# A routed feed-forward kernel: routed rows turned on VectorE, biases moved, batch slots rearranged

## The chip, the cores and the metric

The kernel runs on one core of a Trainium2 chip. The metric is the device time of one launch in microseconds (us), the median of several launches. Five engines run side by side, each with a program of its own, and wait for one another by semaphores: TensorE (PE, with its weight loads as PEld), VectorE (DVE), ScalarE (ACT), GpSimd (POOL) and SyncE (SP, which only issues DMAs here).

## The reference

16 batches of 256 tokens with 256 features pass one block:

```python
x = x + tanh(g_xattn) * xattn(layernorm(x), ctx, ctx)   # 16 heads of 16, full softmax, biases
x = x + tanh(g_ffn) * ffn(layernorm(x))
# ffn
scores = softmax(xf @ w_router)                          # 8 experts, the best 2 of each token
h = silu(xf @ w1[e]) * (xf @ w3[e]);  y = h @ w2[e]      # 256 -> 512 -> 256
out = shared / 3 + 2/3 * sum over the two experts of score * y   # shared: the same form, for all tokens
```

## The kernel before

Everything is fp32; each operand of a large matmul is split into a high part of type fp32r and the rest, and `three` (lines 550 to 552) multiplies high by high, high by rest and rest by high. The program has two stages.

**Attention.** An iteration `i` works on several batches at once: `Eb` = i+4 (layer norm), `A` = i+3 (the projections of q, k and v), `B` = i+1 (row maxima of the scores), `C` = i, `S` = i-1, `S2` = i-2 (output projection, second layer norm), `S3` and `S4` (router, list positions, scatter of the rows into lists of experts in the DRAM tensor `xs_d`). Each iteration has 8 **slots** p = 0..7, and in each of them PE computes scores of one pair of heads for the exponentials (`scores_to_exp`, bank `bank_ss`), scores of another pair for the maxima (`scores_to_max`, `bank_sm`), and then what the table in the section on the change lists. Both score banks are single: the next slot's scores wait for ACT's exponentials (`probs`) and for DVE's maxima (`row_max`) of this slot. `late_pair` says which pair of heads a slot's exponentials belong to: the first LATE slots still serve the batch before. `values` multiplies the probabilities of four heads by v, in four 32-column strips of the array; `turn_...`, `transposes` and `attention_rows` are transposes by matmul with the identity. On each engine `before(p)` and `behind(p)` list what it does ahead of and behind its score work of slot p. The order is written by hand, and each engine keeps it strictly.

**Feed-forward.** 16 tiles of 256 tokens pass the shared expert, and tiles of 256 rows pass the eight routed ones: tiles 0 to 5 are shared, then 34 are routed, then 10 shared. In a tile PE runs `up1` (24 matmuls), for a routed tile `transpose_x(g + 1)` (4 transposes of the next tile's rows `xg` into the bank `psX`; with the one ahead of the loop 35 times), `up3` (24) and `down(g - 1)` (24). The other engines prepare: ACT copies the turned rows to `xg_h` (`x_high_routed`, when up3 has released it), DVE subtracts to get `xg_l` (`x_low_routed`), multiplies the gate (`gated`, into `gg`) and splits again (`g_low`). SP loads the rows of tile u+3 when `xt_ps` says that the rows before are turned; POOL scatters results to `y_d` and converts the next expert's weights (`cut`: lines 1590 and 1594). The last three batches' attention overlaps the first shared tiles.

Of the kernel before, what the change touches and what calls it, by code (L numbers as in the profile page):

```python
# [31 lines left out]
P = 128  # L32
# [7 lines left out]
R = 3  # L40
# [6 lines left out]
LATE = 2  # L47
# [15 lines left out]
SPLIT_AT = NB - 3  # L63
WSZ = 2 * EC * HID + FC * E
# [3 lines left out]
XW = E + 1  # L68

# [59 lines left out]
def build(nc, x, ctxT, gates, wT, bqk, bv, bo, wr, wall, cst, out):  # L129
    with ExitStack() as keep:  # L130
# [84 lines left out]
        with ExitStack() as m:  # L215
# [21 lines left out]
            xg = sb(m, "xg", [P, TS, XW])  # L237
# [54 lines left out]
        xg_in = sem("xg_in"); xs_in = [sem(f"xs_in{i}") for i in range(2)]; xt_ps = sem("xt_ps"); xh_ok = sem("xh_ok"); xl_ok = sem("xl_ok")  # L292
# [60 lines left out]
        def _(sp):  # L353
# [10 lines left out]
            sp.sem_inc(xg_in, EARLY * 16)  # L364
            sp.sem_inc(xt_ps, EARLY)
# [66 lines left out]

            def load_shared(j, done=None):
# [54 lines left out]
            sp.dma_start(xg[:, :, :], parts(xs_d, 0, TR)).then_inc(xg_in, 16)  # L488
            clear_behind(sp, (2, 4, 6), z_done)
            sp.wait_ge(xt_ps, EARLY + 1)  # L490
            sp.dma_start(xg[:, :, :], parts(xs_d, TR, TR)).then_inc(xg_in, 16)
# [52 lines left out]
        def _(pe):  # L544
# [14 lines left out]

            def transpose_x(g):  # L560
                pe.wait_ge(xg_in, g * 16 + 16)
                pe.wait_ge(xl_ok, g)
                for t in range(TS):
                    for k in range(EC):
                        r = pe.transpose(psX[:, k * TR + t * P:k * TR + (t + 1) * P], xg[:, t, k * P:(k + 1) * P], ident)
                r.then_inc(xt_ps, 1)
# [143 lines left out]
            def one(i):  # L710
                A, B, C, S, S2, S3 = (stage(i, k) for k in (3, 1, 0, -1, -2, -3))

                for p in range(PAIRS):
# [5 lines left out]
                    if p == 0 and C and not among_first(C, 1):  # L719
                        turn_max(C, S2)  # L720
                    if p == 0 and S:
                        values(S, 2)
# [11 lines left out]
                    if p == 2 and S:  # L734
                        values(S, 3)
                    if p == 2 and A:
# [27 lines left out]
                    if p == 4 and C:  # L764
                        values(C, 0)
                    if p == 5 and S:
                        if A:
                            pe.wait_ge(xnTl_ok, A.n(1, 1))
                        elif S2:
                            pe.wait_ge(oTl_ok, S2.n(1, 1))  # L770
                        if S2:
                            pe.wait_ge(x2_ok, S2.n(1, 1))
# [1014 lines left out]
```

## Time and profile before

| | us |
|---|---|
| median of 3 runs (lowest to highest) | 838.9 (836.05 to 838.96) |
| the profiled execution's own time | 837.43 |
| its span, first to last instruction | 835.7 |
| PE busy in the span | 787.9 (94%) |
| DVE, POOL, ACT busy | 518.1 (62%), 422.7 (51%), 414.9 (50%) |

The span is 1.7 us shorter than the execution. In rows of the profile, a time is in us from the span's start, `x4` merges four like instructions that follow each other, and a bracket says how long the engine was idle before and what released it. Lines (L550) are those of the kernel before.

### The profile page before, as it was taken

The page shows a single profiled execution, that of the slowest core. Times are in us where ns is not written, and L with a number is a line of the kernel's source. Part 1 is how long each engine was busy: PE and PEld are TensorE (multiplying, and loading weights), DVE is VectorE, ACT ScalarE, POOL GpSimd, SP SyncE.
Part 4 walks back from the last instruction along what each step waited for, and adds up shares of the span by engine and source line. Part 5 has one row for each costly group of instructions (what it writes and reads, how often), then busy time and mean ns, then how long its engine had stood idle before and what let it go on. Part 6 is the DMA issues. An engine that isn't in the chain of part 4 may idle for free.

```text
span 835.7 us, 19335 instructions
## 1 busy us (share of the span) xinstructions
PE 787.9 (94%) x7073; PEld 703.0 (84%) x7074; DVE 518.1 (62%) x1084; ACT 414.9 (50%) x690; POOL 422.7 (51%) x486
## 2 busy tenths in 40 slices
PE   4689999999999998789999999999999999999997
PEld 4556777777777775568999999999999999999996
DVE  6567889998888888847653334333433332346787
ACT  5657777777777776453334433333333333333331
POOL 5533446666666653466672567465836482236000
PEclk9889999999999999689999999999999999999999
DMA  6844556766666652244487233223323312118522
GB/s 219 275 142 164 172 191 212 237 229 216 207 217 215 206 186 84 69 164 153 138 248 270 77 113 115 76 79 122 101 82 96 99 57 69 51 51 325 215 75 76
DMA packets 100542, 127.37 MB, mean 152 GB/s; under 512 B 17664, under 2 KB 82432, under 8 KB 100480
## 3 DMA queue, kind: packets, MB, share of 16 engines
q1 hardware_dynamic: 86336, 80.37, 30.2%
q0 software_dynamic: 14144, 46.19, 16.2%
q8 instruction: 37, 0.61, 0.3%
q14 instruction: 25, 0.20, 0.1%
HBM read 75.36 MB, written 50.91 MB: 151 GB/s over the span
## 4 chain that ended last, share of the span: by engine, by line
PE 80%; DVE 6%; issue 4%; DMA 4%; ACT 3%; POOL 2%; SPq 1%; POOLq 0%; DVEq 0%; ACTq 0%
PE bank L550 9%; PE bank L551 8%; PE bank L552 8%; PE bank L634 6%; PE bank_ss L605 6%; PE bank_sm L550 5%; PE bank_sm L552 5%; PE bank_sm L551 5%; PE bank_ss L550 5%; PE bank_ss L552 5%; PE bank_ss L551 5%; PE bank_sm L618 4%; PE bank L641 3%; DMA y_rows<-xs_d 2%; DVE row_max L1238 2%
## 5 line engine op out<-in xcount | busy, mean ns | idle before, releaser
L1238 DVE TENSOR_REDUCE row_max<-bank_sm 128x4 f32<-128x1024 f32 x124 | 151.6, 1222 | 43.2 <-PE bank_sm L618 42.0
L943 ACT ACTIVATE probs_T<-bank_ss 128x1024 f32<-128x1024 f32 x123 | 126.6, 1029 | 21.3 <-PE bank_ss L605 20.2
L1217 DVE TENSOR_TENSOR gT_l<-gg,gT_h 128x1024 fp32r<-128x1024 f32 x49 | 66.0, 1348 | 89.0 <-ACT gT_h L1074 87.7
L550 PE MATMUL bank_ss<-xg_h,w_h 128*128 128x256 f32 x400 | 115.9, 290 | 0.0
L550 PE MATMUL bank_sm<-xg_h,w_h 128*128 128x256 f32 x400 | 113.5, 284 | 1.0 <-DVE xg_l L1217 1.0
L552 PE MATMUL bank_sm<-xg_l,w_h 128*128 128x256 f32 x400 | 112.9, 282 | 0.0
L551 PE MATMUL bank_sm<-xg_h,w_l 128*128 128x256 f32 x400 | 112.9, 282 | 0.0
L552 PE MATMUL bank_ss<-xg_l,w_h 128*128 128x256 f32 x400 | 112.8, 282 | 0.0
L551 PE MATMUL bank_ss<-xg_h,w_l 128*128 128x256 f32 x400 | 112.7, 282 | 0.0
L550 PE MATMUL bank<-w_h,gT_h 128*128 128x256 f32 x392 | 111.0, 283 | 0.4 <-DVE gT_l L1217 0.4
L551 PE MATMUL bank<-w_h,gT_l 128*128 128x256 f32 x392 | 110.9, 283 | 0.0
L552 PE MATMUL bank<-w_l,gT_h 128*128 128x256 f32 x392 | 110.7, 282 | 0.0
L1644 POOL TENSOR_TENSOR qk_s<-qk_s 128x512 fp32r<-128x512 f32 x32 | 41.8, 1307 | 113.4 <-ACT qk_s L984 113.4
L1217 DVE TENSOR_TENSOR xg_l<-bank,xg_h 128x512 fp32r<-128x512 f32 x34 | 23.5, 693 | 120.9 <-ACT xg_h L1062 120.9
L1068 ACT ACTIVATE sg<-bank_sm 128x512 f32<-128x512 f32 x98 | 53.3, 596 | 67.7 <-PE bank_sm L552 67.7
L1723 POOL DMA_INDIRECT y_d<-y_s,y_rows x68 | 73.0, 1074 | 19.0 <-issue 17.4
L550 PEld LDWEIGHTS bank_sm<-xg_h,w_h 128*128 128x128 f32 x400 | 76.3, 191 | 1.9 <-DVE xg_l L1217 1.4
L984 ACT ACTIVATE qk_s<-bank,bqk_s 128x256 f32<-128x256 f32 (+1 forms) x128 | 53.5, 481 | 47.9 <-PE bank L552 47.9
L551 PEld LDWEIGHTS bank_sm<-xg_h,w_l 128*128 128x128 f32 x400 | 76.4, 191 | 0.0
L552 PEld LDWEIGHTS bank_sm<-xg_l,w_h 128*128 128x128 f32 x400 | 76.3, 191 | 0.0
L551 PEld LDWEIGHTS bank_ss<-xg_h,w_l 128*128 128x128 f32 x400 | 76.2, 191 | 0.0
L1721 POOL TENSOR_TENSOR go<-go 128x1 f32<-128x1 f32 x34 | 11.7, 345 | 127.3 <-ACT y_s L1084 100.7
(200 smaller groups left out, 2079.2 us busy)
## 6 DMA issues: line engine op xcount, KB each, us to landing
qk_d<-qk_s SPq DMA_DIRECT2D x64, 256.0 KB, 2.2
w_raw<-wall POOLq DMA_DIRECT2D x27, 512.0 KB
k<-qk_d SPq DMA_DIRECT2D x48, 256.0 KB
q<-qk_d SPq DMA_DIRECT2D x48, 256.0 KB
xg<-xs_d SPq DMA_DIRECT2D x35, 257.0 KB
y_pairs<-y_d POOLq DMA_DIRECT2D x16, 512.0 KB, 8.8
x<-x SPq DMA_DIRECT2D x16, 256.0 KB, 4.9
c_s<-ctxT SPq DMA_DIRECT2D x16, 256.0 KB, 2.9
```

The lines of the kernel that those rows point to most:

```text
L550: pe.matmul(out, ah, bh, start=first and k == 0, stop=False)
L551: pe.matmul(out, al, bh, start=False, stop=False)
L552: r = pe.matmul(out, ah, bl, start=False, stop=last and k == n - 1)
L605: r = pe.matmul(exp_bank(V.b, pv)[:, par * 512 + half * L:par * 512 + (half + 1) * L], k4[V.slot][own, pv, half * P:(half + 1) * P], q4[V. ...
L634: r = pe.matmul(OT[g % 2][PVW * i:PVW * (i + 1), :], v_s[V.v_slot][:, kc, h, :], pT[:, h % 8, kc * L:(kc + 1) * L], start=kc == 0, stop=kc ...
L943: act.activation(pT[:, 2 * (pv % 4):2 * (pv % 4) + 2, :].rearrange("p h t -> p (h t)"), exp_bank(V.b, pv)[:, :], ACT.Exp, scale=D ** -0.5) ...
L984: r = act.activation(dst.bitcast(F32) if half else dst, bnk[:, oc * L:(oc + 1) * L], ACT.Identity, bias=bqk_s[:, 2 * side + oc:2 * side + ...
L1068: r = act.activation(sg[:, 2 * n:2 * n + 2, :].rearrange("p f t -> p (f t)"), psH1[n][:, :], ACT.Silu)
L1217: return v.tensor_tensor(dst, ps, high.bitcast(F32), ALU.subtract)
L1238: v.tensor_reduce(mx[B.slot][:, :, :].rearrange("p t (r q) -> p r t q", r=2)[:, :, :, p], max_bank(B.b, p)[:, :].rearrange("p (r t k) -> p ...
L1644: po.tensor_tensor(rest, rest.bitcast(F32), high.bitcast(F32), ALU.subtract).then_inc(done, 1)
L1723: po.indirect_dma_start(out=yd, out_offset=bass.IndirectOffsetOnAxis(ap=to[:, t:t + 1].bitcast(U32), axis=0), in_=y_s[:, t, :], in_offset= ...
```

## The change

Four things change.

1. **Routed rows are turned on DVE.** `transpose_x` goes. SP loads a tile by four DMAs of 64 columns each, to 32 partitions each, in pieces of 256 bytes (before: one DMA in pieces of 1028 bytes). DVE turns the tile by one transpose in blocks of 32 by 32 (`turn_rows`) from `xq` to `xrT`, both in SBUF. The rows of w1 and w3 are put in the order that this gives. `x_high_routed` and `x_low_routed` read `xrT` in place of the PSUM bank.
2. **Biases move.** POOL's `add_bias` of batches 11 to 15 stood at the start of iterations 13, 14 and 15; 11 and 12 now stand behind the first scatter of iteration 12, and 13 to 15 behind that of iteration 13.
3. **The slots of a batch are rearranged**, with LATE 3 in place of 2:

| slot | PE behind the scores, before | after |
|---|---|---|
| 0 | turn_max(C), values(S,2) | values(S,1) |
| 1 | logits, project k | turn_max(C), logits, project k |
| 2 | values(S,3), transposes of xn | values(S,2) |
| 3 | project_out, rank | transposes of xn, project_out, rank |
| 4 | values(C,0) | values(S,3) |
| 5 | attention_rows(S), project q | project q, attention_rows(S) |
| 6 | values(C,1), turn_out(S) | values(C,0) |
| 7 | project v, turn_norm(S2) | project v, turn_out(S), turn_norm(S2) |

4. **ACT and DVE follow.** ACT: the copy of the maxima goes from ahead of slot 0's exponential to ahead of slot 1's, the copy of v from ahead of slot 0's to behind it, the two halves of q from around slot 6's to behind slot 5's, the high part of the output from ahead of slot 7's to behind it. DVE: `residual_variance` and `divide` go from ahead of the maxima of slots 5 and 6 to behind them, `residual` and `score_sum`/`score_weights` to behind those of slots 4 and 3. The last batch has one exponential and one `values` more behind the loop.

```diff
-LATE = 2
+LATE = 3
+LAST_X = NB - AHEAD
+BIAS_AT = {LAST_X: (LAST_X - 1, LAST_X), LAST_X + 1: (NB - 3, NB - 2, NB - 1)}
+QD = 32
+FQ = E // (P // QD)
...
+            def load_tile(r):
+                for fg in range(P // QD):
+                    sp.dma_start(xq[QD * fg:QD * (fg + 1), :, :],
+                                 xs_d[bass.ds(r, TR), FQ * fg:FQ * (fg + 1)].rearrange("(t p) d -> p t d", p=QD)).then_inc(xg_in, 16)
...
             def load_routed(u):
                 r = tile_row(u)
-                sp.wait_ge(xt_ps, u + EARLY)
-                sp.dma_start(xg[:, :, :], parts(xs_d, r, TR)).then_inc(xg_in, 16)
+                sp.wait_ge(xt_ok, u + EARLY)
+                load_tile(r)
...
                 up1(g, p)
-                if routed:
-                    transpose_x(g + 1)
                 up3(g, p)
...
+            def turn_rows(g):
+                v.wait_ge(xg_in, g * 64 + 64)
+                v.wait_ge(xl_ok, g)
+                v.transpose(xrT[:, :, :].rearrange("p c (t q) -> p c t q", q=QD),
+                            xq[:, :, :].rearrange("p t (c j) -> p c t j", c=EC)).then_inc(xt_ok, 1)
             def x_low_routed(g):
+                turn_rows(g)
                 v.wait_ge(xh_ok, g + 1)
-                low(xg_l[:, :, :], psX[:, :].rearrange("p (c t) -> p c t", c=EC), xg_h[:, :, :]).then_inc(xl_ok, 1)
+                low(xg_l[:, :, :], xrT[:, :, :], xg_h[:, :, :]).then_inc(xl_ok, 1)
...
-                if S2:
+                if S2 and S2.b <= LAST_X - 2:
                     add_bias(S2)
-                if i == NB - 1:
-                    add_bias(Batch(NB - 2))
-                    add_bias(Batch(NB - 1))
...
                 if S4:
                     scatter(S4, 0)
+                if i in BIAS_AT:
+                    for b in BIAS_AT[i]:
+                        add_bias(Batch(b))
```

PE, the first two slots of an iteration of the attention stage, before (`bank_ss` and `bank_sm` are the scores, `row_max` is turn_max, `probs_T` is values, `wr_s` the router's logits):

```order
L605 MATMUL bank_ss<-q_2,k_2 128x256 x4
L618 MATMUL bank_sm<-k_1,q_1 128x256 x4
L672 MATMUL bank<-consts,row_max 16x128 x2
L634 MATMUL bank<-probs_T,v 32x256 x8
L605 MATMUL bank_ss<-q_2,k_2 128x256 x4
L618 MATMUL bank_sm<-k_1,q_1 128x256 x4
L696 MATMUL bank<-wr_s,xn2T 128x8 x4
```

and the same two slots after, on the same engine:

```order
L608 MATMUL bank_ss<-q_2,k_2 128x256 x4
L621 MATMUL bank_sm<-k_1,q_1 128x256 x4
L637 MATMUL bank<-probs_T,v 32x256 x8
L608 MATMUL bank_ss<-q_2,k_2 128x256 x4
L621 MATMUL bank_sm<-k_1,q_1 128x256 x4
L675 MATMUL bank<-consts,row_max 16x128 x2
L699 MATMUL bank<-wr_s,xn2T 128x8 x4
```

The turning of the maxima has moved past the values and the next slot's scores.

POOL, before, from iteration 14's last scatter to iteration 15's first (`x<-x,gated_bo` is the bias):

```order
L1629 CAST xn_1<-consts 128x2
L1603 TENSOR_TENSOR spare_p<-spare_p 128x1
L1633 DMA xs_d<-xn_1,slot_i 36864x257 x2
L1618 TENSOR_TENSOR x<-x,gated_bo 128x512 x3
L1629 CAST xn_2<-consts 128x2
L1603 TENSOR_TENSOR spare_p<-spare_p 128x1
L1633 DMA xs_d<-xn_2,slot_i 36864x257 x2
```

and after, where the three biases stand in iteration 13:

```order
L1620 TENSOR_TENSOR spare_p<-spare_p 128x1
L1650 DMA xs_d<-xn_0,slot_i 36864x257 x2
L1635 TENSOR_TENSOR x<-x,gated_bo 128x512 x3
L1629 TENSOR_TENSOR rstd<-bn_mv,power 128x2
L1646 CAST xn_0<-consts 128x2
L1620 TENSOR_TENSOR spare_p<-spare_p 128x1
```

The three biases now stand between a first scatter and the root of the second norm, two iterations earlier.

DVE, the loop over routed tiles, before:

```order
L1217 TENSOR_TENSOR xg_l<-bank,xg_h 128x512
L1405 REGISTER_ALU
L1409 TENSOR_TENSOR gg<-sg,bank_ss 128x512 x2
L1217 TENSOR_TENSOR gT_l<-gg,gT_h 128x1024
L1504 REGISTER_ALU
```

and after:

```order
L1413 STREAM_TRANSPOSE xrT<-xq 128x512
L1418 REGISTER_ALU
L1225 TENSOR_TENSOR xg_l<-xrT,xg_h 128x512
L1426 TENSOR_TENSOR gg<-sg,bank_ss 128x512 x2
L1225 TENSOR_TENSOR gT_l<-gg,gT_h 128x1024
```

The transpose heads the loop, right behind the last `gT_l` of the tile before, and the subtraction reads SBUF in place of a bank.

## Rows read from the trace of the kernel before

**Rows 1.** Windows: length, busy PE, PEld, DVE, ACT, POOL, granted clock, DMA, GB/s.
```profile
183.35:304.33 120.98, 118.77 (x1248) 91.28 (x1249) 106.93 (x276) 88.27 (x161) 75.54 (x92) 1.00 0.61 204
...
322.40:325.60 3.20, 3.20 (x26) 1.41 (x24) 2.43 (x6) 1.55 (x3) 0.00 (x0) 0.53 0.02 5
342.50:356.10 13.60, 12.70 (x74) 8.52 (x75) 8.72 (x25) 6.12 (x9) 3.65 (x5) 0.50 0.11 40
...
424.00:734.00 310.00, 308.58 (x2584) 308.18 (x2584) 114.29 (x152) 112.83 (x175) 168.85 (x178) 1.00 0.35 106
```
**Rows 2.** Timeline of PE around the transposes of routed rows: start, us, instruction.
```profile
507.58 0.60 PE L565 MATMUL bank<-consts,xg 128*128 128x128 f32 x4
508.14 0.28 PE L551 MATMUL bank_ss<-xg_h,w_l 128*128 128x256 f32 x1
...
516.64 0.60 PE L565 MATMUL bank<-consts,xg 128*128 128x128 f32 x4
```
**Rows 3.** Timeline of PE, first matmul of two shared tiles in a row.
```profile
766.10 0.28 PE L550 MATMUL bank_sm<-xg_h,w_h 128*128 128x256 f32 x1
...
774.68 0.28 PE L550 MATMUL bank_sm<-xg_h,w_h 128*128 128x256 f32 x1
```
**Rows 4.** Timelines of DVE and ACT in the same routed tile.
```profile
506.56 1.23 DVE L1217 TENSOR_TENSOR gT_l<-gg,gT_h 128x1024 fp32r<-128x1024 f32 x1 [1.96 <-ACT gT_h L1074]
...
511.14 0.60 ACT L1062 ACTIVATE xg_h<-bank 128x512 fp32r<-128x512 f32 x1 [2.20 <-PE bank_ss L552]
511.77 0.69 DVE L1217 TENSOR_TENSOR xg_l<-bank,xg_h 128x512 fp32r<-128x512 f32 x1 [3.99 <-ACT xg_h L1062]
```
**Rows 5.** Timelines at the first routed tiles, and the DMA of 4 MB.
```profile
427.62 1.29 DVE L1409 TENSOR_TENSOR gg<-sg,bank_ss 128x512 f32<-128x512 f32 x2 [1.98 <-PE bank_ss L552]
430.25 0.28 PE L550 MATMUL bank_sm<-xg_h,w_h 128*128 128x256 f32 x1
431.60 1.95 DVE L1217 TENSOR_TENSOR gT_l<-gg,gT_h 128x1024 fp32r<-128x1024 f32 x1 [2.09 <-ACT gT_h L1074]
440.12 1.19 POOL L1713 DMA_DIRECT2D x_all<-x_d  x1
442.96 0.39 SPq L503 DMA_DIRECT2D xg<-xs_d  x1
452.48 0.66 PE L565 MATMUL bank<-consts,xg 128*128 128x128 f32 x4 [1.06 <-DMA xg<-xs_d]
...
x_all<-x_d POOLq DMA_DIRECT2D x1, 4096.0 KB, 16.9
```
**Rows 6.** Timeline of PE in one iteration: starts of slot 1, values in slot 4, slot 5.
```profile
205.26 0.51 PE L605 MATMUL bank_ss<-q,k 64*128 64x256 f32 x4 [0.37 <-issue]
205.60 0.40 PE L618 MATMUL bank_sm<-k,q 63*128 63x256 f32 x4
...
213.72 1.07 PE L634 MATMUL bank<-probs_T,v 128*32 128x256 f32 x16
214.72 0.51 PE L605 MATMUL bank_ss<-q,k 64*128 64x256 f32 x4
215.13 0.50 PE L618 MATMUL bank_sm<-k,q 63*128 63x256 f32 x4
```
**Rows 7.** Timelines of DVE, POOL and PE at the ends of iterations 13 and 14.
```profile
319.18 2.24 DVE L1304 TENSOR_SCALAR xn<-x_s,bn_mv,rstd 128x256 f32<-128x256 f32 x2
321.51 0.63 PE L641 MATMUL bank<-consts,xn 128*128 128x128 f32 x4 [1.63 <-issue]
...
338.63 4.67 DVE L1304 TENSOR_SCALAR xn<-x_s,bn_mv,rstd 128x256 f32<-128x256 f32 x2
339.10 3.71 POOL L1618 TENSOR_TENSOR x<-x,gated_bo 128x512 f32<-128x512 f32 x3
343.40 1.08 PE L641 MATMUL bank<-consts,xn 128*128 128x128 f32 x4 [4.06 <-issue]
```
**Rows 8.** Timeline of DVE at the end of an early iteration.
```profile
138.08 1.70 DVE L1304 TENSOR_SCALAR xn<-x_s,bn_mv,rstd 128x256 f32<-128x256 f32 x2 [0.46 <-POOL rstd L1612]
```

More of the change, by code:

```diff
@@ L718, in one @@
                         scores_to_max(B, p)
-                    if p == 0 and C and not among_first(C, 1):
+                    if p == 0 and S:
+                        values(S, 1)
+                    if p == 1 and C and not among_first(C, 1):
                         turn_max(C, S2)
-                    if p == 0 and S:
-                        values(S, 2)
                     if p == 1 and S3:
@@ L734, in one @@
                     if p == 2 and S:
-                        values(S, 3)
-                    if p == 2 and A:
+                        values(S, 2)
+                    if p == 3 and A:
                         pe.wait_ge(xn_ok, A.n(1, 1))
@@ L788, in one @@
                             project(q_bank(A), 0, oc, xnT_h, xnT_l, q_ps)
+                    if p == 5 and S:
+                        if A:
+                            pe.wait_ge(xnTl_ok, A.n(1, 1))
+                            if among_first(A, R):
+                                pe.wait_ge(qh_ok, A.n(1, 1))
+                        elif S2:
+                            pe.wait_ge(oTl_ok, S2.n(1, 1))
+                        if S2:
+                            pe.wait_ge(x2_ok, S2.n(1, 1))
+                        if among_first(S, 1):
+                            pe.wait_ge(gbo_ok, 1)
+                        if C:
+                            pe.wait_ge(mT_ok, C.n(1, 1))
+                        attention_rows(S)
                     if p == 6 and C:
-                        values(C, 1)
-                    if p == 6 and S:
-                        turn_out(S)
+                        values(C, 0)
                     if p == 7 and A and not among_first(A, R):
@@ L802, in one @@
                         r.then_inc(bo_ps, 1)
+                    if p == 7 and S:
+                        turn_out(S)
                     if p == 7 and S2:
@@ L812, in _ @@
             x13, x14, x15 = (Batch(NB - k) for k in (3, 2, 1))
+            scores_to_exp(x15, PAIRS - 3)
+            values(x15, 1)
             scores_to_exp(x15, PAIRS - 2)
+            logits(x13)
             scores_to_exp(x15, PAIRS - 1)
             values(x15, 2)
-            logits(x13)
             pe.wait_ge(lgc_ok, x13.n(1, 1))
@@ L849, in _, with tile @@
                 up1(g, SHARED)
-                if g == EARLY - 1:
-                    transpose_x(EARLY)
                 up3(g, SHARED)
                 down(g - 1, SHARED)
-            def tile(g, p, before, routed=True):
+            def tile(g, p, before):
                 up1(g, p)
-                if routed:
-                    transpose_x(g + 1)
                 up3(g, p)
@@ L884, in _ @@
             end, = expert(NX - 1, 1, 0, value(T_B, NX - 1, EARLY + 2, EARLY + NT - 2), 1)
-            tile(end, SHARED, 1, routed=False)
+            tile(end, SHARED, 1)
             with pe.Fori(end + 1, end + (NB - 1 - EARLY)) as g:
-                tile(g, SHARED, SHARED, routed=False)
+                tile(g, SHARED, SHARED)
             final = end + (NB - 1 - EARLY)
@@ L1329, in before @@
                         best_two(S3)
-                    if p == 4 and S2:
+                    if p == 4 and S3:
+                        positions(S3, rk_p)
+                    if p == 4 and S2 and not A:
                         residual(S2)
-                    if p == 5 and S2:
-                        residual_variance(S2)
-                    if p == 6 and S:
-                        divide(S)
                     if p == 7 and S2:
```

125 lines of the change are left out of this document (59 added, 66 removed).

## The prediction, made before the changed kernel was run

> **What bounds the kernel.** I read the page's busy times first (they are in the table above): PE works in 787.9 of 835.7 us, the others in 62% or less. Then the same by stretches [rows 1]: in the routed tiles (424 to 734) PE is busy for 308.6 of 310.0 us and DVE for 114.3, so that what PE issues is the time. In six steady attention iterations PE is busy for 118.8 of 121.0 us, but DVE for 106.9 and ACT for 88.3: PE's order sets the time, and DVE has 2.3 us an iteration to spare. In two short stretches the granted clock is half (342.5 to 356.1) or nearly so (322.4 to 325.6). Last come the timelines at these places. Each of them stands at a wait of PE, of 1.63 and of 4.06 us, which the part on the biases takes up.
>
> **Transposes off PE.** Four transposes begin at 507.58, and the second matmul behind them at 508.14. Routed matmuls follow each other at 0.12 us: a tile takes 516.64 - 507.58 = 9.06 us, and (9.06 - 0.44)/72 = 0.12. Without the four, that second matmul would stand at 507.70, so they cost 0.44 us [rows 2]. From the other side: a shared tile with the same 72 matmuls takes 774.68 - 766.10 = 8.58 us [rows 3], which makes it 0.48. I take 0.44; 35 times that is **-15.4** us (at 0.48, -16.8).
>
> **What hides the turning on DVE.** No row shows a DVE transpose. The nearest is DVE's subtraction on as many elements (128x512), 0.69 us [rows 4]; I take that for the transpose. Free, it would be 0; for the other end I take 2.5 us, about four such passes. It starts when `gT_l` ends, 506.56 + 1.23 = 507.79, and ACT wants its result at 511.14, where up3 lets `xg_h` go [rows 4]: 3.35 us of room, 2.9 with the tile 0.44 shorter. Then ACT takes 0.60 and DVE 0.69, up to 512.46, while the next up1 starts 24 matmuls of `down` after up3, at about 513.7. Both ends of the transpose's cost fit, so in the loop it costs 0.
>
> The subtraction itself now has both inputs in SBUF. Such an operation can wait for POOL: `gT_l` took 1.95 us at 431.60 and 1.23 at 506.56 [rows 4, 5], 0.7 more, where POOL was converting weights. The room ahead of up1 is 1.3 us, so this is 0 too, with up to 0.5 at some of the 21 conversions as its worst end. The Trainium skill ("SBUF — State Buffer", the part on the shared port pair) says that a DVE operation with two SBUF inputs, or one in a two-port mode, and a GpSimd operation lock each other out for the whole instruction. By that rule the wait could be a whole conversion instruction, and the transpose might meet it as well; the trace agrees as far as 0.7 us goes.
>
> **The way into the routed tiles.** Here the room is missing. Before, `xg_l` of tile 6 followed `gg`, which ends at 428.91, while its turning was long done; up1 starts at 430.25 [rows 5]. After, the transpose stands between: 0.69 on DVE, 0.60 on ACT, 0.69 on DVE, so `xg_l` ends at 428.91 + 1.98 = 430.9 at best, 431.7 if it waits 0.7 for POOL. Up1 would want it at 430.25 - 0.44 = 429.8. I take **+1.5** (1.1 to 1.9).
>
> Then the load of tile 9. Before, it was issued at 442.96 and let PE go at 452.48, 9.5 us later: POOL had put 4 MB on the same DMA engines at 440.1, which land 16.9 us after it, at 457 [rows 5]. After, the load is issued 2 to 3 us later (behind the transpose of tile 8, which stands behind `gT_l` and three small router steps) and in four times as many pieces. I let it land with the 4 MB, at 457. With 0.69 + 0.60 + 0.69 behind it, up1 of tile 9 can start at 459.0. Before, that up1 stood behind the transposes of 452.48 and 48 matmuls, at 452.48 + 0.44 + 5.76 = 458.7. Less four transposes (1.8) and the wait of 1.06 that go, plus the 1.5 of above, PE asks for it at 457.3 and waits 1.7 us; against the 1.06 removed that is **+0.6**. If the pieces take the load's turn one by one beside the large ones and it ends later, up to +5. The Trainium skill ("DMA: Bandwidth & Descriptors", its table of numbers) says that a transfer wants pieces of 512 bytes or more for the full rate. By it every routed load is slower; elsewhere a whole tile of 8.6 us lies between issue and use, so only the rival on the entry gets its chance from it.
>
> **The biases.** DVE's normalisation is two instructions of 0.37 to 0.41 us. At 338.63 the pair took 4.67 us: it ended when the three biases, 339.10 + 3.71 = 342.81, were done, and PE's transposes waited 4.06 us for it. At 319.18 it took 2.24 us beside one bias, and PE waited 1.63 [rows 7]. After, no bias stands there: **-5.7**. Both waits end in slow clock. In 342.5 to 356.1 PE is busy for 12.7 us at half clock, at full clock 6.4; but DVE has 8.7 us to do in the same stretch [rows 1], so at most 4.0 to 6.4 come back, and I take 4.0. In 322.4 to 325.6 it is 3.2 us of nearly half clock: 1.5. Together **-5.5** (0 if the clock falls all the same). The three biases, now in iteration 13 behind the first scatter, meet small DVE operations with two SBUF inputs (the router's weights, now in slot 3). One bias is 1.24 us (3.71/3): +0.5, from 0 to 3.7. Behind the last batch PE waits for short chains of DVE and ACT, which do not get shorter; of the sum of 10.7 I let **+1.0** be lost there.
>
> **The slots.** In a steady iteration (20.16 us: 120.98/6) the one gap of PE is ahead of slot 1: 0.37 us [rows 6], since ACT copies the maxima ahead of slot 0's exponential. After, that copy waits beside logits and a projection: about -0.4. Against it: the scores behind a `values` take longer. At 214.72 they start 1.00 us after `values`, and the maxima's scores follow 0.41 later, at 205.26 0.34 later [rows 6]; with the like loss at the next step, some 0.17 in all. Before, one slot of eight pays that (the slot behind the gap doesn't), after, slots 1, 3, 5 and 7 do: +0.5. ACT now does both halves of q, four activations, ahead of slot 6's exponential: +0.2. DVE in the short slots (two times scores and one `values`, 0.34 + 0.33 + 1.00 = 1.67 us) has 1.2 us of maxima and up to 0.7 of statistics; the queue catches up in the long ones. Sum +0.3, which I take as 0 (-0.5 to +0.5, times 9). In the three iterations near 138 to 183 the normalisation takes 1.70 us [rows 8], the maxima of slot 7 come late and slot 0 pays some 0.5 us; after, POOL's subtraction of q stands a slot earlier and turn_max has left slot 0: **-1.5**.
>
> **Sum.** -15.4 + 1.5 + 0.6 - 5.7 - 5.5 + 0.5 + 1.0 + 0 - 1.5 = -24.5. The profiled execution took 837.43: 812.9. It stands 1.5 below the median, so 814.4 on the median's scale; I say **814.5**.
>
> **Rivals.**
> - *The clock falls all the same at the end of attention* (a wait of 1 us somewhere else in the last three iterations, where PE has less work than DVE). For it: DVE is busy for 8.7 us there. The 5.5 stay: 820.
> - *The entry jams*: tile 9's load runs on behind the 4 MB, PE stands for 5 us and more, and the clock halves for a while (another 2 to 4). 814.5 + 4 + 3: 821.5. For it: 9.5 us for 257 KB already before; against it: the 4 MB end at 457 in any case.
> - *The slots gain*: the gap goes and nothing comes, and DVE no longer meets POOL: 0.6 an iteration in 12, 807.
> - *Slower*: DVE and ACT cannot hold the short slots. Four slots of 1.67 us stretch to the 2.4 us that maxima plus another DVE step of 0.7 need with their hand-overs, and nothing is given back: 4 x 0.7 = 2.8 us an iteration, in 13 iterations +36: 851. It turns the sign from 24/13 = 1.9 us an iteration. Against it: DVE's load of 17.8 us an iteration (106.93/6) is the same as before and under 20.16.
> - *It does not do what it says*: the transpose is late in every tile and PE waits 0.44 or more for it. That needs over 2.9 + 1.3 us for one transpose, more than my upper end: 830 and up.
>
> **Chances.** My forecast 0.45 (its own range 810 to 819), clock 0.18, entry 0.13, slots gain 0.14, transpose late 0.04, slower 0.06. Range **804 to 828**, which leaves out some 2 in 10. A run of this kernel can't tell less than about 0.5%, 4 us, from no change. Faster by more: 0.92; within: 0.03; slower: 0.05.
>
> **What would show it.** PE without the line of `xg`'s transposes and a period of 8.6 us in routed tiles. DVE's transpose near 0.7 us and ending before ACT's wait for up3. One wait of PE before tile 6 and one before tile 9. Normalisations near 0.8 us a pair in iterations 13 and 14, and full clock from 322 to 356. Steady iterations at 20.2 us, with no gap ahead of slot 1. The prediction is wrong if PE waits for `xg_l` in the loop, if iterations grow by over 1 us, or if the clock falls at other places.

## The result and the profile after

| | before | after |
|---|---|---|
| median, us | 838.2 (836.05 to 838.96) | 828.0 (824.41 to 829.56) |
| ratio, 95% interval | | 0.9876 (0.9838 to 0.9914) |
| span of the profiled execution | 835.7 | 825.8 |

The change is faster by 1.2%, 10.2 us. I had said 814.5, in a range of 804 to 828: the sign is right, the size is less than half of the predicted 24. On a later occasion (e9) the ratio was 0.9917 (0.9904 to 0.993), some 7 us; the two intervals still overlap. Medians in this document are of all executions, while the ratios leave out one execution each of e2 (1471.92 us), e7 (842.51) and e15 (833.82) that lay over 1.5% above the fastest of its kernel.

First come the busy times and stretches of the kernel after; they answer to [rows 1].

```profile
PE 771.2 (93%) x6933; PEld 691.5 (84%) x6934; DVE 546.3 (66%) x1118; ACT 419.2 (51%) x690; POOL 431.1 (52%) x486
...
core 0: us, PE busy (x) PEld busy (x) DVE busy (x) ACT busy (x) POOL busy (x), PEclk, DMA share, GB/s
188.60:308.50 119.90, 119.20 (x1251) 93.00 (x1250) 106.80 (x275) 90.53 (x161) 76.97 (x94) 1.00 0.62 206
322.40:325.60 3.20, 2.64 (x33) 1.55 (x33) 2.89 (x11) 2.35 (x3) 2.09 (x4) 1.00 0.00 0
342.50:356.10 13.60, 11.85 (x127) 8.09 (x128) 12.69 (x45) 9.92 (x16) 6.45 (x9) 1.00 0.24 82
424.00:734.00 310.00, 304.44 (x2501) 303.05 (x2501) 143.82 (x184) 115.48 (x179) 178.31 (x181) 0.99 0.39 106
```

Six steady iterations take 119.90 us, 19.98 each (before 20.16; in the traces of e5 to e16 many of the changed ones take 20.1). The granted clock is full in both stretches at the end of attention where it was 0.53 and 0.50, and the normalisations there take 0.73 us, where they had taken 2.24 and 4.67 [rows 7]. In the routed tiles, where PE was busy for all but 1.4 of 310 us, it now stands still for 5.6. So both large steps of the prediction did what they should, and something else takes the time. To find it, cut both spans at instructions that both kernels have: PE's first, fourth and fourteenth `turn_max`, and the first matmuls of `up1` in tiles 0, 6 and 40 (the first shared one behind the routed). All from timelines of PE, one profiled execution each, us:

| kernel | ahead of 1st turn_max | to 4th | to 14th | to tile 0 | to tile 6 | routed, to tile 40 | rest |
|---|---|---|---|---|---|---|---|
| before | 42.7 | 57.6 | 204.0 | 66.3 | 59.6 | 310.3 | 95.2 |
| after | 43.2 | 63.2 | 202.1 | 56.8 | 63.4 | 301.9 | 95.2 |
| e9, the changed kernel again | 42.5 | 63.3 | 202.7 | 59.2 | 62.2 | 305.0 | 95.2 |
| e1, part 1 alone | 42.2 | 57.6 | 204.1 | 65.7 | 61.9 | 304.6 | 95.2 |
| e2, part 2 alone | 43.0 | 58.3 | 204.8 | 54.5 | 62.3 | 310.2 | 95.1 |
| e3, parts 3 and 4 alone | 42.3 | 62.5 | 202.2 | 54.7 | 62.7 | 310.6 | 95.2 |
| e10, parts 2 to 4 | 42.7 | 63.3 | 202.8 | 59.8 | 59.9 | 310.6 | 95.9 |
| e12, all mended | 43.0 | 62.2 | 202.6 | 56.2 | 60.3 | 295.1 | 95.3 |

DVE's timeline has the normalisation of iteration 14:

```profile
343.04 0.73 DVE L1312 TENSOR_SCALAR xn<-x_s,bn_mv,rstd 128x256 f32<-128x256 f32 x2
```

I had predicted nothing for the first three iterations; they take 5.6 us more. The routed tiles should have given 14.4 and gave 8.4. From the fourteenth turn_max to tile 0 came 9.5 of 10.7 us.

First the start: windows of PE at the low clock (length, busy PE, granted clock, DMA share, GB/s), after and then before.

```profile
43.50:50.30 6.80, 5.47 (x29) 0.50 0.71 230
53.70:60.50 6.80, 5.76 (x30) 0.50 0.20 56
```

```profile
45.50:48.90 3.40, 3.40 (x20) 0.50 0.63 197
52.40:55.80 3.40, 3.40 (x30) 0.50 0.54 156
```

Twice the half clock holds for 6.8 us in place of 3.4. ACT's timeline of the kernel after, and PE's, tell what PE waits for there:

```profile
52.48 0.60 ACT L958 ACTIVATE xnT_h<-bank 128x512 fp32r<-128x512 f32 x1 [1.59 <-PE bank L644]
52.98 1.02 ACT L945 ACTIVATE probs_T<-bank_ss 128x1024 f32<-128x1024 f32 x1
```

```profile
54.05 0.80 PE L608 MATMUL bank_ss<-q,k 64*128 64x256 f32 x4 [1.60 <-ACT probs_T L945]
```

ACT copies `xnT_h` ahead of slot 3's exponential, and the copy waits for PE's transposes, which the change has put behind the scores of that same slot. In a steady iteration slot 3 has project_out and rank to cover this. The first two iterations have neither, and the slot is short.

How long the half clock holds differs between traces of the same start. e5, e6 and e7 do not touch it and ran on one chip; they have 20.5, 13.6 and 10.2 us of half clock there, and the stretch to the fourth turn_max takes 65.1, 63.3 and 62.5 us. At like half clock, 10.2 us, it takes 58.3 with the old slots (e2) and 62.5 with the new (e3, e7). So some 4.2 of the 5.6 us come with the slots at like clock, and the rest with the half clock, of which every trace with the unmended new slots has 10.2 us or more (before and e1 6.8).

Between tiles 1 and 2 PE waits for the normalisation of the last batch, 2.37 us for 0.21 before; e7 takes this up:

```profile
390.11 0.44 PE L644 MATMUL bank<-consts,xn 128*128 128x128 f32 x2 [2.37 <-DVE xn L1312]
```

In iteration 13 stand the three moved biases. POOL, DVE and PE after:

```profile
313.46 3.75 POOL L1635 TENSOR_TENSOR x<-x,gated_bo 128x512 f32<-128x512 f32 x3
```

```profile
312.84 4.40 DVE L1267 TENSOR_TENSOR mask_total<-mask_total,mask 128x8 fp32r<-128x8 f32 x1
```

```profile
317.34 0.25 PE L709 MATMUL bank<-mask_total,counters 128*128 128x16 f32 x1 [2.59 <-issue]
```

One DVE addition of 8 numbers a partition (0.17 us in e3) takes 4.40: it begins 0.62 us ahead of POOL's three operations, under the issue of a scatter on POOL (312.45 to 313.44), and ends 0.03 us behind them. What held it before the biases began is not shown. It does not get its turn between two of them either. PE's rank matmuls read its result. In the trace of after the clock stays full behind this wait. In seven of the nine traces that have both the new slots and the moved biases (e4, e6 to e11) it doesn't: within some 2 us PE is at half clock for 3.4 us (in e9 from 319.2 to 322.6), in five of them once more 14 us later.

Last the routed tiles, first DVE in an undisturbed one:

```profile
497.70 1.23 DVE L1225 TENSOR_TENSOR gT_l<-gg,gT_h 128x1024 fp32r<-128x1024 f32 x1 [3.70 <-ACT gT_h L1080]
498.84 0.71 DVE L1413 STREAM_TRANSPOSE xrT<-xq 128x512 f32<-128x512 f32 x1
```

The transpose takes 0.7 us, PE no longer has the line of `xg`'s transposes, and the period is 8.64 us, for 9.06 in [rows 2]: as predicted. But at 428 and 490 two tiles are slow (tile 6 takes 10.20 us, tile 12 12.55), and four later starts of an expert (tiles 16, 21, 25 and 30) cost 0.5 to 0.8 us each. PE's waits at these two, and the clock behind them:

```profile
428.68 0.36 PE L561 MATMUL bank_sm<-xg_h,w_h 128*128 128x256 f32 x1 [1.84 <-DVE xg_l L1225]
490.85 0.58 PE L561 MATMUL bank<-w_h,gT_h 128*128 128x256 f32 x1 [2.27 <-DVE gT_l L1225]
```

```profile
429.20:432.60 3.40, 3.40 (x18) 0.50 0.62 176
490.60:494.00 3.40, 3.15 (x14) 0.50 0.72 211
```

The wait at 490.85 is followed back through ACT, POOL and SP of the kernel after:

```profile
487.49 0.60 ACT L1090 ACTIVATE y_s<-bank 128x512 f32<-128x512 f32 x1 [6.82 <-DMA y_d<-y_s,y_rows]
487.99 1.05 ACT L1080 ACTIVATE gT_h<-gg 128x1024 fp32r<-128x1024 f32 x1
```

```profile
485.07 0.99 POOL L1740 DMA_INDIRECT y_d<-y_s,y_rows  x1 [0.30 <-issue]
486.06 1.05 POOL L1607 CAST w_h<-w_raw 128x1024 fp32r<-128x1024 f32 x1
487.19 2.52 POOL L1611 TENSOR_TENSOR w_l<-w_raw,w_h 128x512 fp32r<-128x512 f32 x2
...
491.04 1.02 POOL L1740 DMA_INDIRECT y_d<-y_s,y_rows  x1 [0.19 <-issue]
```

```profile
487.64 0.39 SPq L520 DMA_DIRECT2D y_rows<-xs_d  x1
491.59 1.83 SPq L441 DMA_DIRECT2D xq<-xs_d  x4
496.27 0.39 SPq L520 DMA_DIRECT2D y_rows<-xs_d  x1
...
503.59 0.39 SPq L520 DMA_DIRECT2D y_rows<-xs_d  x1
```

The scatter of a tile's results lands; only then may ACT fill `y_s` again (and `gT_h` stands behind it on ACT, `gT_l` and PE's `down` behind that), and only then does SP load the next row numbers, without which POOL can't scatter. It is a circle. At 487.49 ACT has waited 6.8 us for it, since conversions of weights stand ahead of the scatter at an expert's start. From one load of row numbers to the next it is 8.6 us with a conversion in between (487.64 to 496.27) and 7.3 without (to 503.59), while a tile takes 8.64: a delay shrinks by 1.3 us a tile and not at all beside a conversion, and the next expert adds to it. The same loads before:

```profile
489.45 0.38 SPq L509 DMA_DIRECT2D y_rows<-xs_d  x1
497.01 0.38 SPq L509 DMA_DIRECT2D y_rows<-xs_d  x1
503.76 0.38 SPq L509 DMA_DIRECT2D y_rows<-xs_d  x1
```

There it was 7.6 us with a conversion and 6.75 without, under a tile of 9.07: a delay shrank by 1.5 and 2.3 us, and two tiles made it up. So the change took the room from both sides: the tile is 0.43 us shorter and the round 0.6 to 1.0 longer. Summed over the routed tiles, waits after and then before:

```profile
POOL go L1738 <- DMA y_rows<-xs_d: 83.8, 17, 16.4
ACT y_s L1090 <- DMA y_d<-y_s,y_rows: 69.6, 18, 6.8
```

```profile
POOL go L1721 <- DMA y_rows<-xs_d: 26.2, 4, 14.0
ACT y_s L1084 <- DMA y_d<-y_s,y_rows: 12.4, 3, 5.4
```

### The profile page after: what moved, and what is told of

Its sections match the earlier page's. It is cut to its first block, busy times and chain, and to the rows that moved or that the text cites. A ratio compares the mean times of both kernels' runs of the same rounds, so it can differ in the third digit from the quotient of the medians.

```text
span 825.8 us, 19358 instructions
## 1 busy us (share of the span) xinstructions
PE 771.2 (93%) x6933; PEld 691.5 (84%) x6934; DVE 546.3 (66%) x1118; ACT 419.2 (51%) x690; POOL 431.1 (52%) x486
## 4 chain that ended last, share of the span: by engine, by line
PE 56%; POOL 13%; DMA 11%; issue 8%; DVE 6%; ACT 4%; SPq 1%; POOLq 1%; ACTq 0%; DVEq 0%
PE bank_ss L608 6%; PE bank L637 6%; PE bank L561 6%; POOL w_l L1611 6%; PE bank L563 5%; PE bank L562 5%; DMA y_d<-y_s,y_rows 5%; PE bank_sm L621 5%; DMA y_rows<-xs_d 3%; PE bank_sm L561 3%; PE bank L644 3%; PE bank_sm L562 3%; PE bank_sm L563 3%; PE bank_ss L561 3%; PE bank_ss L563 3%
## 5 line engine op out<-in xcount | busy, mean ns | idle before, releaser
L561 PE MATMUL bank_ss<-xg_h,w_h 128*128 128x256 f32 x400 | 113.2, 283 | 0.0
L561 PEld LDWEIGHTS bank<-w_h,gT_h 128*128 128x128 f32 x392 | 75.4, 192 | 4.4 <-DVE gT_l L1225 4.4
L608 PEld LDWEIGHTS bank_ss<-q,k 64*128 64x128 f32 x492 | 38.2, 188 | 45.7 <-ACT probs_T L945 29.5
L563 PEld LDWEIGHTS bank_ss<-xg_l,w_h 128*128 128x128 f32 x400 | 76.4, 191 | 0.0
```

Source lines behind the costliest of these rows:

```text
L561: pe.matmul(out, ah, bh, start=first and k == 0, stop=False)
L563: r = pe.matmul(out, ah, bl, start=False, stop=last and k == n - 1)
L608: r = pe.matmul(exp_bank(V.b, pv)[:, par * 512 + half * L:par * 512 + (half + 1) * L], k4[V.slot][own, pv, half * P:(half + 1) * P], q4[V. ...
```

## The experiments

Eighteen runs, on five chips: e1 to e4, e5 to e8, e9 to e12, e13 to e16, and e17 with e18. Ratios are to the kernel before on the same chip, with 95% intervals. A time in the table above is one trace's.

### Parts of the change

e1 is part 1 of the change alone, e2 part 2 alone, e3 parts 3 and 4 alone, e10 parts 2 to 4; their edits are those of the numbered list in the section on the change.

> The kernel before with part 1 alone: routed rows turned on VectorE; biases and slots as before. Theory A (the routed stage loses its gain at the starts of experts, whatever stands in attention): period of a routed tile 8.64 us, but a slow tile at the entry (+3.4) and 4 to 8 us at the starts of experts, so about -7 us against before (831). Theory B (what I had predicted for this stage): -15.4 + 2.1, about -13 us (825).

Measured: 832.8 us, 0.9936 (0.9919 to 0.9953), 4.8 us. The routed tiles gain 5.7 us, the entry loses 2.3: theory A, if with less than its 7 us.

> The kernel before with part 2 alone: the biases of batches 11 to 15 moved, slots and routed tiles as before. Theory A: the waits of 1.63 and 4.06 us and the half clock behind them go (-11.2), the three biases in iteration 13 cost +2.7 and a little is lost behind the last batch: -7 to -9 us (830). Rival B (the slot rearrangement is needed for the clock to stay full): the waits go, the clock still falls somewhere in the last three iterations: -3 to -5 us.

Measured: 830.45, 0.9905 (0.9883 to 0.9926), 7.1 us. To tile 0 it gains 11.8 us where the waits and the half clock stood, and loses 2.7 on the way to tile 6. The clock stays full there without the new slots: theory A.

> The kernel before with parts 3 and 4 alone (slots rearranged, exponentials a slot later). Theory A (it is this part that lengthens the first iterations): +3 to +4 us in the first three iterations, -0.18 us in each of 9 steady iterations, +1 to +2 behind the last batch: together +2 to +5 us (841 to 843), and one more step of half clock near 42 to 59 us than before. Rival B: the slots are neutral at the start and gain 0.2 us an iteration: -2 us (836).

Measured: 831.53, 0.9928 (0.9911 to 0.9944), a gain of 6.0 us: both theories were wrong. The start costs 4.9 us, as A said. But the stretch to tile 0 gains 11.6, as much as moving the biases does, with the biases where they were. Its DVE and POOL show why: the normalisation is through before the bias begins.

```profile
320.01 0.73 DVE L1318 TENSOR_SCALAR xn<-x_s,bn_mv,rstd 128x256 f32<-128x256 f32 x2
```

```profile
321.27 1.29 POOL L1634 TENSOR_TENSOR x<-x,gated_bo 128x512 f32<-128x512 f32 x1
```

> The kernel before with the slots and the biases changed (parts 2 to 4), routed tiles as before. Alone the biases gave -7.1 us and the slots -6.0. Theory A (both remove the same two waits of PE at 321 and 343 and the same half clock, so that the second adds nothing, and the three biases in iteration 13 now cost 3.5 us): less than either alone, -3 to -5 us (834). Rival B (the gains add up): -13 us (825).

Measured: 834.47, 0.9961 (0.9949 to 0.9973), 3.0 us: less than either alone, as A said. Parts 2 and 3 remove the same two waits; together they pay for it twice, at the start (5.7 us) and in iteration 13, so that the stretch to tile 0 gains 6.5 us and not 11.7. In that stretch stand the rank's wait (2.56 us) and, behind it, twice 3.4 us of half clock, which neither part has alone.

### Single mends of the changed kernel

e9 is the changed kernel itself. It shares its chip with e10 to e12 alone; the chips of e4 and of e5 to e8 have no run of the unedited changed kernel, so those runs can only be set beside e9's ratio and beside each other.

> The changed kernel itself, unchanged. The four runs before this one (ratios 0.991 to 0.992) all stand above the 0.9876 measured for the changed kernel on another occasion, and in their traces the middle iterations take 20.17 us where the first run of the changed kernel had 19.98. Theory A: the gain of the change itself varies by 0.3 to 0.4% between occasions (waits for DMAs in the routed tiles), so here it lies anywhere from 0.987 to 0.993, and only runs of one occasion may be compared. Rival B: it is 0.9876 again, and each of the three edits (turning earlier, rstd earlier, xnT_h later) cost 3 us.

Measured: 830.78, 0.9917 (0.9904 to 0.993). It fits theory A, 10 us on one occasion and 7 on another, though the intervals overlap by 0.001. The trace has PE's wait for tile 9's load longer (2.54 us, and the half clock behind it), and 2.4 us more in the stretch to tile 0, where its two stretches of half clock stand behind the rank's wait.

e4:

```diff
-                moved(sp, y_st, u * 32)
+                moved(sp, now_ok, u + EARLY)
...
+                load_rows(u)
                 load_routed(u + 3)
-                load_rows(u)
...
+                po.tensor_tensor(to_now[:, :], to[:, :], none[:, :], ALU.add).then_inc(now_ok, 1)
```

The first hunk is in `load_rows`: the load waits for POOL's copy of the row numbers and no longer for the landed scatter. The second is SP's order.

> The changed kernel; SP loads the row numbers of routed tile u+1 into y_rows as soon as POOL has copied those of tile u to a second small buffer, ahead of the load of x, and no longer when the scatter of tile u has landed. Theory A (the circle scatter, load of row numbers, scatter takes 8.0 of 8.64 us, so that a delay at an expert's start is not made up; ACT waits with y_s, and gT_h, gT_l and PE's down behind it): the circle shortens by 2 to 2.5 us, ACT's waits of y_s for y_d fall from 69.6 us to under 30, the slow tile at 490 us (+3.9) and most of the five expert starts (+0.5 each) go: -4 to -6 us against the changed kernel (823). Rival B (POOL's conversions ahead of the scatter hold it anyway): under 1 us.

Measured: 824.08, 0.984 (0.9823 to 0.9857). Its routed tiles take 297.6 us, where those of the change took 301.9 to 305.1 in six traces; ACT's waits for `y_s` on the landed scatter fall from 69.6 to 35.9 us, not quite to the 30 expected, and of the expert starts at tiles 16 to 30 none costs anything. Theory A; the round that it puts at 8.0 us is 7.3 in the rows above.

e5, the biases back where they were (part 2 undone):

> The changed kernel with part 2 undone: the biases of batches 11 to 15 stand again where they stood before. Theory A (the rearranged slots alone already keep the normalisation clear of the biases, as the run with the slots alone shows; in iteration 13 the three biases now hold up DVE's small router operations, and PE's rank matmuls wait 2.59 us for them): the wait of 2.59 us goes, none of 1.63 or 4.06 comes back, the clock stays full: -2.5 to -4 us against the changed kernel (824.5). Rival B (the moved biases are what keeps the clock full at 322 to 356): the waits of 1.6 and 4.1 us and the half clock return: +8 us (836).

Measured: 831.19, 0.9909 (0.9894 to 0.9923); e6 to e8, on the same chip, give the same. The stretch to tile 0 is 57.2, against 59.6 to 60.3 in these three. The rank's wait is gone and the waits of 1.63 and 4.06 us don't come back; of half clock one stretch of 3.4 us is left (352.8 to 356.2). So A holds in place, while the time shows nothing. In the profiled execution the start took 65.1; e11, which has the changed kernel's start, took 65.0 with as much half clock, so that is no effect of the edit.

e6:

```diff
             g_low(4)
+            turn_rows(EARLY)
             gated(5)
-            x_low_routed(EARLY)
+            x_low_routed(EARLY, turned=True)
```

> The changed kernel; DVE turns the rows of tile 6 ahead of the gate of tile 5 and not behind it (they have lain in xq since 412). Theory A: xg_l of tile 6 ends 0.7 to 1.3 us earlier, the wait of 1.84 us falls to under 1, and with it the half clock of 427.9 to 431.3 (1.56) goes: -2.3 to -3 us. Rival B (POOL's conversions lock xg_l, which took 1.75 us there, so that its end moves little; or a short wait is enough for half clock): -0.7 us or less.

Measured: 830.42, 0.9914 (0.9901 to 0.9927), no change against the others of this chip and against e9. The wait at tile 6 and the half clock are gone (tile 5 takes 8.60 us, 10.51 in e5). But PE now comes to tile 9 earlier, whose rows land when they land:

```profile
457.45 0.39 PE L561 MATMUL bank_sm<-xg_h,w_h 128*128 128x256 f32 x1 [3.77 <-DVE xg_l L1225]
```

Neither theory saw it: what is gained ahead of a load with a fixed landing is given back at it, here with a half clock on top (tile 9 takes 10.22).

e7:

```diff
+            root(bmv2, rstd2, var2_ok, x15, rstd2_ok)
             cut(1, 0, which=(1,))
-            root(bmv2, rstd2, var2_ok, x15, rstd2_ok)
```

> The changed kernel; POOL computes rstd of the last batch ahead of the second part of the weight conversion, not behind it. Theory A (PE's wait of 2.37 us at 390 for xn of the last batch comes from POOL's order: the conversion of 383.96 to 388.5 stands ahead of rstd and locks five small DVE operations): the wait goes, -2 to -2.4 us. Rival B (xn stands behind xg_l on DVE, which waits for ACT and PE): under -1 us.

Measured: 831.59, 0.9916 (0.9899 to 0.9933), no change. PE still waits 1.42 us there. In the first trace it had been 2.37, but in those of e9 and e6, without this mend, it is 1.10 and 0.17, so one trace can't price it. POOL's `rstd` is ready early now, and the conversion that follows it holds up the normalisation itself, 2.65 us where it takes 0.74:

```profile
388.03 2.89 POOL L1611 TENSOR_TENSOR w_l<-w_raw,w_h 128x512 fp32r<-128x512 f32 x2
```

```profile
388.42 2.65 DVE L1312 TENSOR_SCALAR xn<-x_s,bn_mv,rstd 128x256 f32<-128x256 f32 x2
```

e8:

```diff
+RAMP_TO = 2
...
-                    if p == 3 and A:
+                    if p == 3 and A and i >= RAMP_TO:
                         from_bank(xnT_h, T0, xnT_ps, A, q_ps, A.n(2), xnTh_ok)
...
+                    if p == 3 and A and i < RAMP_TO:
+                        from_bank(xnT_h, T0, xnT_ps, A, q_ps, A.n(2), xnTh_ok)
```

The first place is in `before(p)`, ahead of the exponential, the second in `behind(p)`.

> The changed kernel; in iterations up to 1 ACT copies xnT_h behind slot 3's exponential, not ahead of it. Theory A (the +3.0 us of iterations 1 and 2 against before come from this order: the exponential stands behind a copy that waits for PE's transposes at the end of the same slot, 1.60 us of wait of PE twice, and a step of half clock): iterations 1 and 2 together 39.7 -> 37.5 us, -2 to -3 us in all. Rival B (it comes from one exponential fewer in the first iteration, whatever ACT's order): the wait moves to another slot, within 0.5 us.

Measured: 831.01, 0.9915 (0.9901 to 0.9929), within the noise of the others. In place the start falls from 63.3 (e6; 62.5 in e7) to 60.9, and 3.3 us over the kernel before are left. Part of the fall is clock: e8 has 6.8 us of half clock there, e6 13.6. At like half clock the mend is worth some 1.1 us: 61.4 with it (e15, e16) and 62.5 without (e3, e7) at 10.2 us, 62.2 (e12) and 63.3 (e6, e9) at 13.6. That is half of what A said, or less.

e11:

```diff
-            po.dma_start(x2a[:, :, :], x2_d.rearrange("b p d -> p b d")).then_inc(x2_in, 16)
+            def load_x2(e):
+                for b in range(2 * e, 2 * e + 2):
+                    po.dma_start(x2a[:, b, :], x2_d[b]).then_inc(x2_in, 16)
...
+                load_x2(e)
```

The call stands at the start of expert e.

> The changed kernel; the 4 MB of x_all are loaded in 16 pieces of 256 KB, two at the start of each expert, and not in one transfer at 440. Theory A (the load of tile 9 is late because its packets take turns with the 4 MB): the load lands within 4 us and the tiles 8 to 10 take 8.64 us each, -0.5 to -3.5 us against the changed kernel of this occasion. Rival B (the pieces at every expert's start disturb the scatter and the loads there, where SP and POOL are already late): +1 to +4 us.

Measured: 831.75, 0.9932 (0.9914 to 0.995), against 0.9917 for e9. Tiles 8 to 10 take 8.64 us each, so the load of tile 9 was late because of the 4 MB. The gain is given back in tile 16 (12.88 us) and later, where PE waits for `gT_l`: the circle.

### All mends together, and one left out

e12 is the changed kernel with the mends of e4 to e8 and e11.

> The changed kernel with part 2 undone, the row numbers loaded early, xnT_h later in the first iterations, tile 6 turned early, rstd ahead of the conversion, and x_all in pieces. Theory A (the five losses are separate and each is mended where it stands): -3.5 (iteration 13), -4.3 (row numbers), -2 (first iterations), -2 to -4 (entry with tile 9), 0 to -2 (rstd): -12 to -15 us against the changed kernel of this occasion, 0.970 to 0.975 of before. Rival B (time gained at one place is given back at the next, as tile 6's at tile 9): -6 to -8.

Measured: 817.75, 0.9765 (0.9752 to 0.9778), 13.0 us below the changed kernel on the same chip and 19.8 below before. PE waits for `gT_l` twice for over 0.2 us in the routed tiles, 0.23 at 517.07 and, the longer:

```profile
526.28 0.39 PE L564 MATMUL bank<-w_h,gT_h 128*128 128x256 f32 x1 [0.32 <-DVE gT_l L1230]
```

> The kernel with all mended, but with the row numbers loaded as in the change (behind the landed scatter). Theory A (the circle scatter, row numbers, scatter is the largest loss of the routed tiles): PE waits for gT_l again at the starts of experts, +4 to +7 us against the full set (823). Rival B (the late load of x_all and the entry were what put the circle out of step): under +1.5 us.

Measured: 826.02, 0.9873 (0.9851 to 0.9896), 6.6 us above e16. Routed tiles 302.7 against 294.8; tile 16 waits 3.26 us for `gT_l` and takes 13.61. Theory A.

> The kernel with all mended, but with the biases moved as in the change. Theory A: PE's rank matmuls wait 2.6 us in iteration 13, +3 to +4 us against the full set (821). Rival B (what is lost in iteration 13 is made up behind the last batch, where PE waits for others anyway): under +1 us.

Measured: 820.65, 0.9808 (0.9781 to 0.9834), 1.2 us above e16; the intervals overlap. In the trace the stretch to tile 0 is 58.3 against 56.2, with the rank's wait of 2.59 us but no half clock behind it. So 1 to 2 us here, between the theories, and the time alone can't tell it from nothing.

> The kernel with all mended, but with x_all loaded in one transfer of 4 MB. Theory A (with tile 6 early, tile 9 waits the longer for its load, as in the run with the early turning, where tiles 8 and 9 took 12.57 and 10.22): +3.5 to +5.5 us against the full set (822). Rival B (the wait is worth only what the changed kernel showed in its first trace, 0.5): +0.5.

Measured: 823.04, 0.9827 (0.9801 to 0.9853), 3.6 us above e16; routed 300.1, with tiles 8 and 9 of 12.72 and 10.21. Theory A, at its lower end.

> The kernel with all mended once more, as the control of this occasion: 0.9765 of before again, within 0.002, if its gain does not hang on the occasion as that of the changed kernel does (0.988 and 0.992).

Measured: 819.4, 0.9786 (0.9758 to 0.9815), 0.0001 outside the bound, with the intervals overlapping.

e17:

```diff
+            if C and C.b == 0 and p >= LATE - 1:
+                return C, p - LATE + 1
+            if S and S.b == 0 and p < LATE:
+                return (S, PAIRS - LATE + p) if p else (None, 0)
```

> The kernel with all mended; the exponentials of the first batch run two slots late as before, and three slots late from the second batch on. Theory A (the first stretch pays for an exponential that the first iteration no longer hides): the stretch from the first turn_max to the fourth falls from 61.4 to 62.3 us to 60 to 61, time -1 to -1.5 us. Rival B (the stretch pays for waits inside short slots without work of S2, whatever the lateness): no change within 0.5 us.

Measured: 816.21, 0.9765 (0.9745 to 0.9785). The start is 63.7, not shorter, with 17.0 us of half clock; e18, on the same chip, takes 62.1 with 13.6. So rival B: nothing speaks for the lateness of the first batch, though one trace with another clock can't exclude a part of a microsecond, and the batch's last two exponentials stand three slots late even here. What makes up the remaining 3 us at like clock (61.4 in e16, 58.3 in e2) is open.

e18 has the four loads of x ahead of the row numbers on SP, as in the change, and is e12 otherwise.

> The kernel with all mended, but SP issues the four loads of x ahead of the load of the row numbers, as in the change; the row numbers still wait only for POOL's copy of those before. Theory A (what counts is that the load no longer waits for the landed scatter): the routed tiles take the same 295 us, time within 0.5 us of the full set. Rival B (what counts is SP's order, since the four loads wait for DVE's transpose and take 1.83 us to issue): the routed tiles take 298 to 302 us, +3 to +7 us.

Measured: 822.24, 0.9823 (0.9791 to 0.9855). It is 6.0 us above e17, which ran on the same chip and has e12's routed tiles (294.7). Routed tiles 302.9. Of the 8 us above e12's, 4.2 stand at tiles 6 and 7, whose loads this edit does not touch (tile 7's rows landed at 433.8, in e12 at 430.0, since the last scatters of attention had been late). The rest stands at starts of experts: tiles 16, 25 and 26 cost 2.5, 1.0 and 0.7 over a period, in e12 0.5 and 0, in e13 5.0, 0.8 and 0.7. So both halves of the mend count, the wait and the order: neither theory alone. Its six executions spread from 819.65 to 828.03 us; the traced one took 824.29.

## Why the prediction was wrong

**Right.** Without the turning PE's tile is 0.43 us shorter (9.07 to 8.64, 0.44 predicted), and on DVE it takes 0.70, inside its room. The biases' waits and the half clock behind them go: 9.5 of 10.7 us. The entry to tile 6 waits 1.84 us (1.5 predicted). Steady iterations stay within the bounds (-0.18 in this trace, next to nothing in those of e5 to e16). No part was slower on its own, and the rival "slower" did not come.

In the first trace 14.6 us are missing (24.5 predicted, 9.9 in the span): 5.6 at the start, 5.4 at starts of experts, 1.6 of half clock at tile 6, 1.7 more between tiles 0 and 6, 1.2 in the stretch to tile 0, and small ones; the load of tile 9 gave 1.3 back.

**"So in the loop it costs 0"** is the first step that failed: 5.4 us (6.0 over the period at tiles 12, 16, 21, 25 and 30, against 0.6 before), in e9 6.2. I looked for the cover of the transpose on DVE and found it. What I did not follow was the release it gives. SP's loads now wait for DVE, not for PE, and are four, 1.83 us of issue against 0.38; behind them in SP's order stand the row numbers on which the scatter turns. The trace of before had the signs: ACT's longest wait of 5.4 us for the landed scatter, POOL's of 14.0 for row numbers. Before, the circle had 2.3 us of slack, after, 1.3, and none beside a conversion: so a delay lasts. Of this the shorter tile takes 0.43 by itself, and no run separates it. e4 and e13 show the circle (4 to 8 us), e18 that wait and order share it.

**"Early iterations: -1.5"** looked at the wrong ones. The ten iterations up to the fourteenth gave 1.9. The first three cost 5.6, for which the sum has no term: I had held the new slots against the steady iteration alone, where projections and rank cover ACT's copy. e3 puts 4.9 us on the slots, 4.2 of them at like half clock; the copy's order is worth some 1.1 (e8 and e12 to e16), e17 finds nothing in the lateness, and 3 us stay open.

**"Biases in iteration 13: +0.5"**, range to 3.7, came near the upper end: 2.59 us of PE's wait, by e5 and e14 worth 1 to 3. I had taken one bias for the length of the lock, and it was all three. In e9 and e10 two stretches of half clock follow it, so the rival "the clock falls all the same" came in part, behind a wait that the change itself made. The gain of 11.2 was right in size (e2: 11.8), but the slots alone bring it too (e3: 11.6), so it says nothing for moving the biases.

**"Load of tile 9: +0.6"**: tiles 8 and 9 stand 0.6 us over the period in the first trace, 1.3 before, so it came as -0.7; the load landed at 454.5 and not with the 4 MB at 457. In e9 they stand 4.3 over, which is +3.0: the bound of +5 held, and one value can't be given.

**"Behind the last batch: +1.0"** and the entry's **"+1.5"** came as 3.8 together, and 1.6 of half clock follow the wait of 1.84 us. I had counted such clock at [rows 7] and not here.

Of the rivals "the entry jams" (821.5) is nearest, and 828 lay at the edge of my range, which had room for one thing going wrong and not for four. No single term explains the miss; the two largest, the start and the circle, are the ones that I had at nothing.

## What to carry to other kernels

Where an operation changes engines, follow its release as well as its cost: who issues on that semaphore, what stands behind it in that queue, and whether a closed circle (store, index load, store) runs through it with less slack than the period. Check a rearranged pipeline in its first iterations, where the work that covers a wait is still missing. Compare a start only at like granted clock: here traces of the same code differ there by 2.6 us. Two parts aimed at one wait don't add up, and a mend ahead of a fixed landing or a full circle shows nothing until the next limit goes too: here five of six mends (e5 to e8, e11) gave nothing alone that times could tell, and all six together 13 us.

## What the hardware showed that I had not expected

- A DVE operation with two SBUF inputs can wait for a whole run of POOL operations: 4.40 us for 8 elements beside three biases of 1.25. Beside two subtractions of a conversion it got its turn between them:

```profile
385.15 1.27 DVE L1276 TENSOR_TENSOR products<-one_hot,list_pos 128x32 f32<-128x32 f32 x1
385.09 2.52 POOL L1611 TENSOR_TENSOR w_l<-w_raw,w_h 128x512 fp32r<-128x512 f32 x2
```

  What decides between the two is not shown. The Trainium skill ("SBUF — State Buffer", section "Who interferes with whom") says that such an operation contends with a GpSimd instruction that reads SBUF, and that whoever issues first keeps the ports that the two engines share for the whole instruction. The trace agrees beside the conversion and shows three instructions beside the biases.
- One DVE transpose of 128x512 fp32 in 32 by 32 blocks takes 0.70 us, as a subtraction on as many elements does.
- A stretch of 3.4 us at half clock cost 1.6 us at tile 6 (10.20 against 8.64). It followed PE's wait of 1.84 us there after, and those of 1.78 in e4 and 1.81 in e11; none followed those of 1.85 in e9 (clock 1.00 from 429.9 to 433.3), 1.79 in e1, 1.77 in e5 and 1.80 in e8. At the start the same code was at half clock for 10.2, 13.6 or 20.5 us.
- The changed kernel gained 10 us on one occasion and 7 on another. Between the two traces stand 3.7 us at the load of tile 9, by when a DMA landed, and 2.4 in the stretch to tile 0, with half clock in one and not in the other.
